# Small loads moved to ScalarE's queue, adjacency issued directly behind x, and first masks made between ScalarE's copies

## The reference, cut to what matters

```python
def _L0_gnn_ref(input, adj, W, a):
    h = jnp.matmul(input, W)
    a1 = a[:Fout, 0]
    a2 = a[Fout:, 0]
    f1 = jnp.einsum('bnf,f->bn', h, a1)
    f2 = jnp.einsum('bnf,f->bn', h, a2)
    e = jax.nn.leaky_relu(f1[:, :, None] + f2[:, None, :], negative_slope=ALPHA)
    logits = jnp.where(adj > 0, e, NEG_BIG)
    attention = jax.nn.softmax(logits, axis=1)
    h_prime = jnp.matmul(attention, h)
    return jax.nn.elu(h_prime)
...
x = x + _L0_gnn_ref(_layernorm(x, axis=-1), adj, L0_gnn_W, L0_gnn_a)
```

## Time and profile before

| | |
|---|---|
| median of 3 runs | 1091.12 us (1091.12 to 1091.54) |
| profiled execution, its own time | 1090.56 us |
| its span in the trace | 1088.8 us |
| mean granted TensorE clock | 0.989 of full speed |
| PE, DVE, ACT, POOL busy | 94%, 69%, 69%, 35% of the span |

### The profile page before, as it was taken

The page is one execution under the profiler, slowest core; times in us unless marked ns, Lnnn a source line. Parts: engine busy times, 40 slices in busy tenths (PEclk is TensorE's granted clock), DMA queues, the critical chain, the costliest instruction groups (busy, mean ns, idle before and its releaser), DMA issues. The chain is left out here.

```text
span 1088.8 us, 20069 instructions
## 1 busy us (share of the span) xinstructions
PE 1018.7 (94%) x6404; PEld 740.5 (68%) x6445; DVE 750.3 (69%) x2196; ACT 747.4 (69%) x1152; POOL 380.5 (35%) x470
## 2 busy tenths in 40 slices
PE   4999999787999989899999999999999999999997
PEld 3566666455677778588888888885566666666666
DVE  3789999687554365788899899754446666666535
ACT  4988888685565456788888888866665565656550
POOL 4134888888571504556665662010000000000000
PEclk8999999899999999999999999999999999999999
DMA  9967877894266755333323232201025545545101
GB/s 304 359 247 294 305 268 246 314 346 145 75 203 212 221 169 152 94 95 88 90 83 93 86 91 60 58 14 75 1 65 170 173 145 169 180 155 161 53 20 32
DMA packets 81099, 166.27 MB, mean 153 GB/s; under 512 B 11247, under 2 KB 37469, under 8 KB 79965
## 3 DMA queue, kind: packets, MB, share of 16 engines
q1 hardware_dynamic: 71788, 145.52, 40.4%
q0 software_dynamic: 8192, 16.79, 5.3%
q10 hardware_dynamic: 1008, 2.62, 0.7%
HBM read 110.24 MB, written 54.66 MB: 151 GB/s over the span
## 5 line engine op out<-in xcount | busy, mean ns | idle before, releaser
L2463 PEld LDWEIGHTS eY<-Vo,dGW 128*128 128x128 f32 x1024 | 132.5, 191 | 54.2 <-issue 52.8
L600 POOL DMA_INDIRECT sorted_x<-V,AT_I x128 | 126.2, 986 | 55.5 <-issue 37.3
L2463 PE MATMUL eY<-Vo,dGW 128*128 128x128 f32 x1024 | 134.3, 276 | 0.2
L2446 PE MATMUL eU<-XTN,V 128*128 128x512 f32 x256 | 130.9, 593 | 0.8 <-PEq L2350 0.8
L2454 PE MATMUL eU<-H,V 128*128 128x512 f32 x256 | 131.1, 594 | 0.0
L792 PE MATMUL O<-Y,HS 128*128 128x512 f32 x256 | 128.6, 623 | 1.5 <-DVE Vo L1177 1.0
L2027 POOL DMA_INDIRECT W<-sorted_y,ROW_I x96 | 97.4, 1014 | 62.9 <-PE f_T L2110 24.6
L2546 ACT ACTIVATE H<-eU,bn 128x512 f32<-128x512 f32 x128 | 99.5, 778 | 25.4 <-PE eU L2446 16.2
L2137 PEld LDWEIGHTS f_O<-f_XN,f_PT 128*128 128x128 f32 x896 | 106.7, 192 | 13.0 <-DVE X L2248 10.5
L2137 PE MATMUL f_O<-f_XN,f_PT 128*128 128x128 f32 x896 | 109.8, 276 | 3.9 <-DVE X L2248 2.2
L2643 DVE TENSOR_TENSOR dGW<-H,WBC 128x512 f32<-128x512 f32 x80 | 55.3, 692 | 82.8 <-PE eY L2463 82.7
(11 more groups left out here) (332 smaller groups left out, 2046.9 us busy)
## 6 DMA issues: line engine op xcount, KB each, us to landing
XTN<-in_adj SPq DMA_DIRECT2D x64, 512.0 KB, 5.8
entries<-in_adj SPq DMA_DIRECT2D x64, 512.0 KB, 3.5
masks<-NMW SPq DMA_DIRECT2D x8, 2048.0 KB
f_MK<-masks SPq DMA_DIRECT2D x60, 256.0 KB, 2.8
sorted_y<-zero SPq DMA_DIRECT2D x36, 256.0 KB
NMW<-sorted_x SPq DMA_DIRECT2D x25, 256.0 KB, 2.8
sorted_y<-NMW SPq DMA_DIRECT2D x25, 256.0 KB, 2.6
X<-in_x SPq DMA_DIRECT2D x8, 512.0 KB, 7.4
```

The source lines that it names most:

```text
L600: g_.indirect_dma_start(sorted_x, bass.IndirectOffsetOnAxis(ap=AT_I[b % 2][:, kt:kt + 1], axis=0), XR[b % 2][:, t * P:(t + 1) * P], None). ...
L2446: pe.matmul(U1[j % 2][:, :], V1[:, e * P:(e + 1) * P], XTN[:, b * N + q * HALF:b * N + (q + 1) * HALF], start=True, stop=True).then_inc(u1 ...
L2463: i = pe.matmul(Y[q][:, t * P:(t + 1) * P], GW[:, j % 2, t * P:(t + 1) * P], Vo[:, e * P:(e + 1) * P], start=(e == 0 and t == 0), stop=(e ...
```

## The change

The six small loads are issued by ScalarE, ahead of its wait, so SP issues adjacency directly behind x. GpSimd's three selects on pick move to the second program, and the memset of 1/128 from the second to the first; waits follow (before_ready counts the three selects and the select on before). ScalarE's conversions 3 to 7 of graph 0 are put between and behind the copies of H.

```diff
@@ -162,14 +162,6 @@
                 sp.dma_start(X[:, 0:N].rearrange("p (t d) -> p t d", t=NT),
                              x[0].rearrange("(t p) d -> p t d", p=P)).then_inc(x_loaded[0], 16)
-                sp.dma_start(Wg[:, 0:P], p["L0_gnn_W"]).then_inc(gat_loaded, 16)
-                sp.dma_start(A12[:, :], p["L0_gnn_a"].rearrange("k o -> o k").to_broadcast([P, 2 * P])
-                             ).then_inc(gat_loaded, 16)
-                sp.dma_start(Wr0[:, :], p["L0_ffn_Wr"]).then_inc(gat_loaded, 16)
-                sp.dma_start(br0[:, :], p["L0_ffn_br"].rearrange("(o e) -> o e", o=1).to_broadcast([P, E])
-                             ).then_inc(gat_loaded, 16)
-                for k, n in enumerate(("gamma", "beta")):
-                    sp.dma_start(gb[:, k:k + 1], p[f"L0_ffn_{n}"].rearrange("(h o) -> h o", o=1)).then_inc(gat_loaded, 16)
                 entries = XTN[:, :].bitcast(I32)
@@ -187,14 +179,20 @@
-                v = pick[0:3 * E, :].rearrange("r (e m) -> r e m", e=E)
-                for k in range(3):
-                    nc.gpsimd.affine_select(out=v, in_=v, compare_op=ALU.not_equal, fill=1.0, base=-k * E,
-                                            pattern=[[-1, E], [0, P]], channel_multiplier=1).then_inc(cstep, 1)
-                    pool.wait_ge(cstep, c.next())
+                nc.gpsimd.memset(Vo[:, 0:P], 1.0 / P).then_inc(cstep, 1)
+                c.next()
+                pool.wait_ge(cstep, c.now())
 
             @block.scalar
             def _(act):
+                nc.scalar.dma_start(Wg[:, 0:P], p["L0_gnn_W"]).then_inc(gat_loaded, 16)
+                nc.scalar.dma_start(A12[:, :], p["L0_gnn_a"].rearrange("k o -> o k").to_broadcast([P, 2 * P])
+                             ).then_inc(gat_loaded, 16)
+                nc.scalar.dma_start(Wr0[:, :], p["L0_ffn_Wr"]).then_inc(gat_loaded, 16)
+                nc.scalar.dma_start(br0[:, :], p["L0_ffn_br"].rearrange("(o e) -> o e", o=1).to_broadcast([P, E])
+                             ).then_inc(gat_loaded, 16)
+                for k, n in enumerate(("gamma", "beta")):
+                    nc.scalar.dma_start(gb[:, k:k + 1], p[f"L0_ffn_{n}"].rearrange("(h o) -> h o", o=1)).then_inc(gat_loaded, 16)
                 act.wait_ge(cstep, 8)
                 nc.scalar.activation(most[:, 0:1], minus1[:, :], ACT.Exp)
@@ -600,7 +598,11 @@
-                g_.memset(EL[:, 0:P], 1.0 / P).then_inc(g_ready, 1)
+                v = pick[0:3 * E, :].rearrange("r (e m) -> r e m", e=E)
+                for k in range(3):
+                    g_.affine_select(out=v, in_=v, compare_op=ALU.not_equal, fill=1.0, base=-k * E,
+                                     pattern=[[-1, E], [0, P]], channel_multiplier=1).then_inc(before_ready, 1)
+                    pool.wait_ge(before_ready, k + 1)
                 root(0)
@@ -752,7 +754,7 @@
-                    pe.wait_ge(before_ready, 1)
+                    pe.wait_ge(before_ready, 4)
@@ -768,6 +770,8 @@
                     if c == 0:
                         pe.wait_ge(f1r_ready, b + 1)
+                    if g == 0:
+                        pe.wait_ge(before_ready, 3)
@@ -792,12 +796,12 @@
-                pe.wait_ge(g_ready, 2)
+                pe.wait_ge(g_ready, 1)
...
-                pe.wait_ge(g_ready, 3)
+                pe.wait_ge(g_ready, 2)
@@ -1002,10 +1006,14 @@
                 for h in range(2):
                     copy_xnt(0, h)
-                for k in range(3):
-                    copy_h(0, k)
-                for t in range(BY_VECTOR, NT):
-                    convert(0, t)
+                convert(0, 3)
+                convert(0, 4)
+                copy_h(0, 0)
+                convert(0, 5)
+                copy_h(0, 1)
+                copy_h(0, 2)
+                convert(0, 6)
+                convert(0, 7)
@@ -1350,7 +1358,6 @@
-                dve.wait_ge(g_ready, 1)
                 v.tensor_scalar(EL[:, P:2 * P], EL[:, 0:P], gb[:, 1:2], float(P), ALU.mult, ALU.mult).then_inc(g_ready, 1)
```

## The result

| | before | after |
|---|---|---|
| median (10 runs each, side by side) | 1091.90 us (1090.35 to 1094.30) | 1095.84 us (1093.81 to 1099.22) |
| ratio after / before | | 1.0037, 95% interval 1.0028 to 1.0047: 3.1 to 5.1 us slower |
| profiled execution, own time / span | 1090.56 / 1088.8 us | 1099.22 / 1097.4 us |
| mean granted clock of it | 0.989 | 0.987 |

The changed kernel is slower, where 2.3 us faster was forecast; both the sign and the range (1086.9 to 1091.3) are wrong. All ratios here leave out three executions that ran far longer than the rest (1201.69 us of the kernel before, 2923.31 of the one with adjacency in loads of 64 rows, 2709.15 of the one with six tiles issued in the second program).

A forecast was written before the change was run, and what follows sets the result against it. The prediction took two chains meeting at the first relu, with the masks setting its time, to bound the kernel. Its terms, -1.9 - 0.5 - 0.2 + 0.3 = -2.3 us, gave a median of 1088.8 us, range 1086.9 to 1091.3.

The forecast's parts named there:

- Small loads on ScalarE's queue: First program: beta issued earlier by ScalarE; -0.5 us, bounds -2.5 (nothing in the way) and +4.6 (each row waits for adjacency's).
- The first relu sets the end: Attention loop: whatever brings ScalarE's first relu, at 23.72 us, earlier should bring the end earlier by as much.
- Masks between the copies: ScalarE, second program: masks 3 to 7 earlier, H chain 0.41 us later, first relu sooner; -1.9 us, bounds -2.2, -1.4.
- Adjacency behind x: SP's queue, first program: adjacency issued from about 1.29 us lands in time for masks 3 and 4; cost 0, bounds 0 and 0.7.
- Constant memset: POOL's memset moves into the first program, so VectorE starts the second program 0.23 us earlier; -0.2 us.
- pick in the second program: Second program's start: POOL's first select collides with VectorE's first scaling; +0.3 us, bounds 0 and 1.18.
- Rival 4: Small loads take turns with adjacency row by row, landing at 13.0 us and holding VectorE; +2.8 us, 1093.9; chance 0.08.

The follow-up runs named there:

- the split version: Changed kernel with br, gamma, beta on SP's queue ahead of x, Wg, A, Wr on ScalarE's, and GpSimd's selects waiting for VectorE's scaling: ratio 1.0009 to the kernel before.
- the gate of five loads: Changed kernel with br issued last on its own semaphore, so VectorE's first wait needs five small loads instead of six: ratio 1.0019 to the kernel before.
- the selects that wait: Changed kernel with the small loads back on SP's queue and GpSimd's three selects on pick waiting for VectorE's first scaling: ratio 0.9984 to the kernel before.
- br apart: Changed kernel with five small loads back on SP, br on ScalarE's queue with its own semaphore, and selects waiting for VectorE's scaling: ratio 0.9984 to the kernel before.

## Why the prediction was wrong

**The failed step is *Small loads on ScalarE's queue*:** taken -0.5, measured +5.60 (VectorE's first wait 8.37 to 13.97), 1.0 beyond its own upper bound. The upper bound's count was the right one: 32 rows in the line of four loads, each paid with about one adjacency row. What it was short by is the size of a turn and the issue. With the measured 0.18 a row (taken 0.16; or 36 packets of 0.16) it is 5.8 us instead of 5.1, and the issue of beta was at 3.61, not 3.33, as ScalarE issued at 0.56 us each and not at SP's 0.50; 3.61 + the 4.56 of before + 5.8 = 13.97. That adjacency beside them is what holds the small loads is shown (held back, they land in 3.4 us; ahead of it in one queue, in 4.2 to 4.5). That the engines take turns is what fits best, not shown against service in order of issue. What misled was the choice between the bounds. The indirect gathers are single loads beside traffic of another kind; they show what one load loses (0.9 us), not what four loads in a line lose. The prediction had already counted the line, 32 rows, and then set it aside for a row that has no line. The Trainium skill's rule in "DMA: Bandwidth & Descriptors", Queues, rings and completion order, that a DMA engine takes turns between its queues, would have given the sign. The trace agrees with it: 466 packets of each queue in 8.0 to 12.5 us, and 1.43 us for each load of 8 rows an engine.

The other steps:

- *The first relu sets the end*: held. The relu's shift over 1092 lies within the measured interval in 12 of 13 comparisons (the changed kernel twice, eleven others; the split version's on its very edge; an interval is some 2 to 3 us wide, so smaller losses behind the head would not show), from -2.55 (only the order, 0.9977 in 0.9974 to 0.9996) to +5.30 (only the loads, 1.0049 in 1.0040 to 1.0068). The exception is the gate of five loads, +3.35 or 1.0031 against 1.0010 to 1.0028.
- *Masks between the copies*: right in mechanism. -1.50 here and 2.08 alone, against -1.9 (bounds -2.2, -1.4). The H chain lost 0.32 (0.41 forecast); the rest is the matmul spacing, at the slow bound for all sixteen in the changed kernel.
- *Adjacency behind x*: 0, and 0 measured, but only because the head was 5 us late. No run has this order of issues with an early head. In four with an early head and adjacency issued later than here, tiles 3 and 4 bind (0.23 to 3.57 us).
- *Constant memset*: -0.2, measured -0.18.
- *pick in the second program*: +0.3, measured +0.90, near the upper of its bounds 0 and 1.18. (The prediction's 1.18 is 3.53 / 3; one select takes 1.08.) Selects and root power delayed nothing, as argued.
- *Rival 4* was the outcome at a chance of 0.08. Its +2.8 us was short by 1.0 of landing, 0.6 of port and 0.4 of order, which is where the other misses went.

Of what was tried the best are the order alone (0.9985), the selects that wait (0.9984) and that with br apart (0.9984), which these intervals don't separate. So what the change has to gain lies in ScalarE's order; the queue move is what has to be left out.

**Left open.** Whether the DMA engines take turns or serve in order of issue: a run that issues the small loads at another pace than adjacency's would tell. What one turn holds, where one load's share of an engine fits best. Why rows of half the length cost 0.127 us and not 0.09. Why Wr takes 6.5 us on ScalarE's queue in the split version. Why the gate of five loads ends somewhat lower than its head says. And what decides the spacing of the first mask matmuls where the granted clock is 1.00 (below).

## What to carry to other kernels

Loads of many tiny rows that gate a program belong ahead of a saturated stream of long rows in the same queue, not beside it in another: here, beside loads of 128 long rows, each row of theirs on a DMA engine cost a long row's time, so count rows per engine over the whole line of such loads, whatever their bytes. An experiment that shrinks the stream's loads shrinks what is issued ahead as well; work out both theories' landing before it is built. When a bound rests on a count of this kernel's own and the milder row comes from an operation with another shape of traffic, stay near the count. Before a wait is pulled ahead of a barrier, look at who reaches the barrier last then, SP's DMA issues (0.5 us each) among them; and where POOL and VectorE start together, let the long one wait for the short one.

## What the runs showed of the hardware that was not expected

- In the changed kernel, the first sixteen matmuls of logits(0) start 0.105 us apart (26.62 to 28.19, 15 gaps) while the window 26 to 28 us has a granted clock of 1.00. In the earlier trace rows the first ten have 0.057 and only later ones, at a granted clock of 0.64 over the window, 0.106, the spacing of 1.2 GHz. Idle time ahead doesn't tell them apart: before the transpose of F1, TensorE idled 1.80 us in the changed kernel and 1.81 with the order alone. Four profiles start at 0.057: before, only the loads, the order alone and br apart, this one until its granted clock falls at about 20.4. The other ten start at 0.105 (worth up to 0.8 us of head). In two of them the granted clock explains it: it is 0.50 when the version with six tiles in the second program begins logits(0), and with the selects waiting it is 0.66 over 20 to 21 us, so it falls to 1.2 GHz at about 20.3, where the matmuls begin. In the other eight it reads 1.00, and no single edit goes with them.
- A fall of the granted clock inside the attention loop costs 1.3 to 1.7 us. With none between 50 and 155 us the loop takes 240.13 and 240.23, with one 241.44 to 241.87 (five profiles), with two 243.34 to 243.55 (five). Where it falls differs: from 120 us in one profile of the changed kernel, from 60 and 92 in the other. That is more than some of the effects measured here, and why one profiled execution's total is not compared.
- Issuing one 0.5 KB load from ScalarE takes 0.5 to 0.9 us beside SP's issues, and 1.32 us once, beside sixteen of them.
- Loads of 64 rows x 4 KB moved 215 GB/s in 8 to 10 us, loads of 128 rows 392, at the same DMA share of about 1.
